# One-core attention and mixture-of-experts block: earlier value blocks, keys in three passes, and small moves between engines

## The reference, cut to what matters

```python
q = (queries @ Wq + bq); k = (keys @ Wk + bk); v = (values @ Wv + bv)   # keys = values = the context
scores = where(causal, -inf, q @ k.T);  attn = softmax(scores * scale)
x = x + (attn @ v) @ Wo + bo            # queries = layernorm(x)
# second block, on u = layernorm(x)
qkv = layernorm(u) @ qkv_weight.T;  ao = softmax(causal(q @ k.T * scale)) @ v
h1 = u + ao @ proj_weight.T
logits = layernorm(h1) @ router_weight          # top 2 of 8, capacity 1280 an expert
moe = scatter_add(prob * (gelu(token @ w1) @ w2))
out = x + (h1 + moe)
```

## Time and profile before

| | us |
|---|---|
| median of 3 runs | 1589.51 |
| lowest, highest | 1587.81, 1590.07 |
| profiled execution | 1583.6 |
| its span | 1581.8 |
| mean granted TensorE clock | 0.976 of full speed |

### The profile page before, as it was taken

The page is one execution under the profiler, slowest core; times in us unless marked ns, Lnnn a source line. Parts: engine busy times, 40 slices in busy tenths (PEclk is TensorE's granted clock), DMA queues, the critical chain, the costliest instruction groups (busy, mean ns, idle before and its releaser), DMA issues. The chain is left out here.

```text
span 1581.8 us, 31078 instructions
## 1 busy us (share of the span) xinstructions
PE 1477.9 (93%) x11056; PEld 1309.9 (83%) x11057; DVE 920.4 (58%) x1741; ACT 712.1 (45%) x1425; POOL 833.5 (53%) x951
## 2 busy tenths in 40 slices
PE   8798899999999999899859998999999899999986
PEld 6577788888888888788749988998999789899876
DVE  3767677777778767788665464433233653453361
ACT  2445545555555555565415453433233643342341
POOL 2445455556666556698725566542542855354332
PEclk9999999999999999999959999999999999999999
DMA  7212211122222111222223343432422534333222
GB/s 262 66 63 75 88 59 50 63 72 82 75 75 67 62 66 64 75 93 88 99 80 91 78 88 100 104 83 54 107 58 48 135 90 103 81 94 54 32 35 25
DMA packets 64400, 125.96 MB, mean 80 GB/s; under 512 B 13369, under 2 KB 13785, under 8 KB 63724
## 3 DMA queue, kind: packets, MB, share of 16 engines
q1 hardware_dynamic: 45932, 93.81, 18.2%
q0 software_dynamic: 17920, 29.31, 10.9%
q10 hardware_dynamic: 384, 0.61, 0.1%
HBM read 89.14 MB, written 46.27 MB: 86 GB/s over the span
## 5 line engine op out<-in xcount | busy, mean ns | idle before, releaser
L1503 PEld LDWEIGHTS hidden_ps<-gT,w 128*128 128x128 f32 x2880 | 350.3, 192 | 11.3 <-ACT hT L1408 3.9
L1503 PE MATMUL hidden_ps<-gT,w 128*128 128x256 f32 x2880 | 352.9, 284 | 7.0 <-ACT hT L1408 3.5
L1530 PE MATMUL expert_ps<-w,hT 128*128 128x512 f32 x1440 | 341.0, 396 | 8.1 <-DVE og L1458 8.1
L1530 PEld LDWEIGHTS expert_ps<-w,hT 128*128 128x128 f32 x1440 | 271.9, 191 | 65.9 <-DVE og L1458 8.9
L1283 POOL TENSOR_TENSOR w<-raw,w 128x1024 fp32r<-128x1024 f32 x62 | 152.9, 2514 | 261.5 <-ACT w L1277 261.5
L1433 DVE TENSOR_TENSOR hT<-gl,hT 128x512 fp32r<-128x512 f32 x160 | 125.9, 795 | 249.0 <-ACT hT L1408 225.3
L1406 ACT ACTIVATE gl<-hidden_ps 128x512 f32<-128x512 f32 x160 | 95.7, 598 | 326.6 <-PE hidden_ps L1503 258.6
L1387 POOL DMA_INDIRECT out_dram<-og,idx x78 | 126.0, 1616 | 72.8 <-DVE og L1458 44.0
L1458 DVE TENSOR_SCALAR og<-expert_ps,kept 128x512 f32<-128x512 f32 x80 | 59.3, 749 | 156.4 <-PE expert_ps L1530 147.4
L1416 ACT ACTIVATE gT<-yk 128x256 fp32r<-128x256 f32 x160 | 67.0, 419 | 127.7 <-DVE yk L1444 118.7
L1375 POOL DMA_INDIRECT xg<-normed_tokens,idx x78 | 86.4, 1108 | 56.2 <-POOL idx L1370 30.9
(11 more groups left out here) (184 smaller groups left out, 3079.5 us busy)
## 6 DMA issues: line engine op xcount, KB each, us to landing
raw<-L_ffn_moe_w_dram SPq DMA_DIRECT2D x64, 512.0 KB
normed_tokens<-h SPq DMA_DIRECT2D x128, 65.0 KB
xa<-x_dram SPq DMA_DIRECT2D x32, 256.0 KB, 2.7
xc<-x_dram SPq DMA_DIRECT2D x32, 256.0 KB, 3.0
attended_rows<-x SPq DMA_DIRECT2D x32, 256.0 KB, 2.1
fx<-attended_rows SPq DMA_DIRECT2D x128, 64.0 KB
out_dram<-fx SPq DMA_DIRECT2D x128, 64.0 KB
fx<-qkv_rows_dram SPq DMA_DIRECT2D x1, 1536.0 KB, 6.7
```

The lines of the kernel that those rows point to most:

```text
L1503: last = pe.matmul(pH[:, q, f * W:(f + 1) * W], w1[p][l][:, k, cols], xT[g.s % 2][r][:, k, :], start=k == 0 and n == 0, stop=k == KT - 1 a ...
L1530: last = pe.matmul(pY[:, k, :], hT[par][l][:, f, k * P:(k + 1) * P], w2[p][r][:, f, :], start=f == 0 and n == 0, stop=f == FT - 1 and n == 2)
```

## The change

Nine things are changed.

1. The keys are made in three fp32r passes. ScalarE copies the high halves of each of the four parts of cT and rk into the buffers that later hold wqkv and wpj, VectorE makes the low halves, and TensorE issues 96 matmuls. This stands ahead of the statistics and norms of the first tiles on VectorE and ScalarE.
2. A table VALUES sets where the value blocks are made: blocks 0 and 1 in step 2 (0 ahead of q, 1 ahead of "s"), block 2 in step 3, blocks 3 and 4 in step 4 (3 ahead of "xt", 4 ahead of "s"). Their banks are 4, 5, 4, 6, 5. SyncE sends them one step later, now behind xc.
3. A job that takes banks 0 or 1 from scores waits for the first half of pr alone.
4. In the odd steps 5 to 13 ScalarE copies pT ahead of xT_hi, and VectorE makes the low half of xT, in the steps before these, behind the sums of the exponentials.
5. The pieces of wpj and wqkv are prepared in the other order, wpj first.
6. In steps 15 to 38 VectorE transposes q of the second attention ahead of the softmax sum and its reciprocal.
7. In the steps after 38 v_spread is made by ScalarE (4 copies with a scale), not by GpSimd.
8. The choice of tiles 26 to 30 moves from step 50 to step 49, behind the maxima.
9. The low half of the last piece of the first expert's first weights moves from VectorE in step 50 to GpSimd in the expert phase.

```diff
-LATE_LOW = {LATE + 11: 6, LATE + 12: 7}
+LATE_LOW = {LATE + 11: 6}
 VB = -(-S * SK // P)
-CHOICES = {..., STEPS - 2: (26, 31, None)}
+VALUES = {2: ((0, 0), (1, 2)), 3: ((2, 2),), 4: ((3, -1), (4, 2))}
+VALUE_BANKS = (4, 5, 4, 6, 5)
+CHOICES = {..., STEPS - 3: (26, 31, None)}
...
+    cTh = [w[:, :, 0:S * SK] for w in wqkv]
...
         def bank_free(pe, kind, t, j=0):
             for old, t_old, j_old in ousted[kind, t, j]:
-                pe.wait_ge(*read_out[old](t_old, j_old))
+                if old == "s" and kind != "s" and place[kind, t, j] < 2:
+                    pe.wait_ge(s["shifted"], 2 * t_old + 1)
+                else:
+                    pe.wait_ge(*read_out[old](t_old, j_old))
...
# SyncE
                 if 0 < i < NT - 2:
                     load_x(i + 2)
-                b = i - 3
-                if 0 <= b < VB:
+                t = tile(i, LP)
+                if t is not None:
+                    need(sp, s["x2_done"], t - 1)
+                    sp.dma_start(xc[:, t % 2, :], x2d[row0(t):row0(t) + P, :]).then_inc(xc_in[t % 2], 16)
+                for b, _ in VALUES.get(i - 1, ()):
                     sp.wait_ge(s["val_done"], b + 1)
                     for seq, row, key, n in value_rows(b):
                         sp.dma_start(va[key:key + n, seq, :, :]..., stage[row:row + n, :]).then_inc(va_in[b], 16)
...
# GpSimd
                 f = tile(i, FF + 2)
-                if f is not None:
+                if f is not None and i <= LATE:
                     pool.wait_ge(s["v_kept"], f + 1)
...
+                if isinstance(c, int) and c == 0 and i == 5:
+                    low(pool, 0, 0, CH - 1)
...
# ScalarE
+            for k in range(KT):
+                act.wait_ge(keys_in[k], 32)
+                act.activation(cTh[0][:, k, :], cT[:, k, :], ACT.Copy)
+                act.activation(wpj[0][:, k, :], rk[:, k, :], ACT.Copy).then_inc(s["key_hi"], 1)
             for t in range(2):
                 norm_x(t)
...
+                turned_first = i % 2 == 1 and LP <= i <= FF
+                if not turned_first:
+                    normed_high(i)
...                                        # here the copies of pT
+                if turned_first:
+                    normed_high(i)
...
+                f = tile(i, FF + 2)
+                if f is not None and i > LATE:
+                    act.wait_ge(s["v_kept"], f + 1)
+                    act.wait_ge(s["v_spread"], f)
+                    need(act, s["o2_mm"], f)
+                    for b in range(4):
+                        last = act.activation(vbd[:, :, b, :], vn[:, f % 2, :]..., ACT.Copy, scale=blocks[:, b:b + 1])
+                    last.then_inc(s["v_spread"], 1)
...
# VectorE
-            for t in range(2):
-                stats_x(t)
+            for k in range(KT):
+                dve.wait_ge(s["key_hi"], k + 1)
+                dve.tensor_tensor(cTh[1][:, k, :], cT[:, k, :], cTh[0][:, k, :].bitcast(F32), ALU.subtract)
+                dve.tensor_tensor(wpj[1][:, k, :], rk[:, k, :], wpj[0][:, k, :].bitcast(F32), ALU.subtract)\
+                   .then_inc(s["key_lo"], 1)
+                if k % 2 == 1:
+                    stats_x(k // 2)
...
-                b = i - 2
-                if 0 <= b < VB:
+                for b, _ in VALUES.get(i, ()):
                     dve.wait_ge(s["val_mm"], b + 1)
                     dve.wait_ge(bias_in, 32)
                     if b > 0:
...
                     dve.transpose(hq, parts(bank("qkv", f, 0))).then_inc(s["q_turned"], 1)
+                f = tile(i, FF + 2)
+                if f is not None and i <= LATE:
+                    dve.wait_ge(s["exp2"], f + 1)
+                    need(dve, s["shared2"], f - 1)
+                    chained(dve.tensor_reduce(den2[:, :], p2, X, ALU.add))
+                    dve.reciprocal(rec2[:, f % 2, :], den2[:, :]).then_inc(s["rec2_done"], 1)
...
# TensorE
+            def values(i, stage):
+                for b, at in VALUES.get(i, ()):
+                    if at == stage:
+                        pe.wait_ge(wv_in, 16)
+                        bank_free(pe, "val", b)
...
             for k in range(KT):
-                pe.wait_ge(keys_in[k], 32)
-                for n in range(8):
...
+                pe.wait_ge(s["key_hi"], k + 1)
+                for n_pass, (w, c) in enumerate(PASSES):
+                    if n_pass == 1:
+                        pe.wait_ge(s["key_lo"], k + 1)
+                    for n in range(8):
...
```

More of the change, by code:

```diff
@@ L182, in psum_jobs, with values @@
     fz, fq, fs, fo, ft, fr = (tile(i, FF + n) for n in range(6))
-    jobs = [("xt", tx, 0, 1)] + [("pt", tp, j, 0) for j in range(4)] + [("p2t", fo, 0, 0)]
+    def values(stage):
+        return [("val", b, 0, 1) for b, at in VALUES.get(i, ()) if at == stage]
+    jobs = values(-1) + [("xt", tx, 0, 1)] + [("pt", tp, j, 0) for j in range(4)] + [("p2t", fo, 0, 0)]
+    jobs += values(0)
     if i % 2 == 0:
@@ L201, in own_bank @@
         return 2
-    if kind in ("pt", "val"):
+    if kind == "val":
+        return VALUE_BANKS[t]
+    if kind == "pt":
         return 4 + j % 2
@@ L1027, in _ @@
                         dve.reciprocal(rec[:, t % 2, heads], den[:, heads]).then_inc(s["rec_done"], 1)
+                if i % 2 == 0 and LP <= i + 1 <= FF:
+                    later(i + 1)
                 if i > FF:
@@ L1045, in turn_z @@
                 transposes("zt", f, z).then_inc(s["zt_mm"], 1)
+            def values(i, stage):
[3 more added lines that the diff above has]
+                        bank_free(pe, "val", b)
+                        n = min(P, S * SK - P * b)
+                        for k in range(KT):
+                            last = pe.matmul(bank("val", b)[0:n, :], cT[:, k, P * b:P * b + n], rv[:, k, :],
+                                             start=k == 0, stop=k == KT - 1)
+                        last.then_inc(s["val_mm"], 1)
             def count_places(a, b, batches):
@@ L1063, in _ @@
             for k in range(KT):
-                pe.wait_ge(keys_in[k], 32)
-                for n in range(8):
-                    m, h = divmod(n, 2)
-                    last = pe.matmul(bank("key", n)[:, 0:HC], rk[:, k, m * P:(m + 1) * P], cT[:, k, h * HC:(h + 1) * HC],
-                                     start=k == 0, stop=k == KT - 1)
-                    if k == KT - 1:
-                        last.then_inc(s["key_mm"], 1)
+                pe.wait_ge(s["key_hi"], k + 1)
[3 more added lines that the diff above has]
+                    for n in range(8):
+                        m, h = divmod(n, 2)
+                        final = k == KT - 1 and n_pass == 2
+                        last = pe.matmul(bank("key", n)[:, 0:HC], wpj[w][:, k, m * P:(m + 1) * P],
+                                         cTh[c][:, k, h * HC:(h + 1) * HC], start=k == 0 and n_pass == 0, stop=final)
+                        if final:
+                            last.then_inc(s["key_mm"], 1)
             pe.wait_ge(small_in, 16)
@@ L1129, in _ @@
                     count_places(*COUNTS[i])
-                b = i - 2
-                if 0 <= b < VB:
-                    pe.wait_ge(wv_in, 16)
-                    bank_free(pe, "val", b)
-                    n = min(P, S * SK - P * b)
-                    for k in range(KT):
-                        last = pe.matmul(bank("val", b)[0:n, :], cT[:, k, P * b:P * b + n], rv[:, k, :],
-                                         start=k == 0, stop=k == KT - 1)
-                    last.then_inc(s["val_mm"], 1)
+                values(i, 2)
                 if tq is not None:
```

45 lines of the change are left out of this document (25 added, 20 removed).

## The result

| | kernel before | changed kernel |
|---|---|---|
| median of 8 runs | 1588.11 us | 1593.71 us |
| lowest, highest | 1585.10, 1590.35 | 1590.84, 1594.78 |
| profiled execution, span | 1583.6, 1581.8 | 1593.6, 1591.8 |

The changed kernel is slower: ratio 1.0032, interval 1.0022 to 1.0042, some 5.1 us. The forecast was 3.4 us faster, and the time lies just outside its range. The two spans differ by 10.0 us, twice what the medians do, since the profiled execution of the kernel before is a short one, 4.5 us under its median. A comparison of the two traces has to be brought down by some 4.5 us, and the traces do not say where.

The account below looks back on a forecast made before the run. TensorE, busy 93%, bounds the kernel, so only its stops pay. Early +9.4, steady −8.6, late −1.6, end −2.6 make −3.4 on 1583.6 us; with 5.9 us to the median carried over, 1586.1 us, range 1580 to 1593.

Parts of the forecast that it names:

- The new wait, twice: Steps 2 and 4: VectorE's second value addition waits for the first block's DMAs; stalls of 6.3 and 8.2 us.
- rivals A and B: A: values' DMAs don't hold VectorE, sum −19.4, 1570 us, chance 0.08. B: transfers land sooner, −5.7, 1583.8, chance 0.17.
- The start: From the keys to s of the first value step: keys done 2.1 us sooner, but s 4.2 us later.
- rival C: TensorE falls to the lower clock behind each new stop: +7.7, sum +4.3, 1593.8 us, chance 0.17.
- The half shift: Early steps: q's first half waits for half of pr only, which gives 0.79 us each time.
- the early part: All up to the second attention's begin: start, two stalls and what comes back, +9.4 us in sum.
- The steady steps: Second attention: q's transposition moved ahead of reduction and reciprocal lets all 15 pv waits go, −8.6 us.
- rival D: The reorder gives half, as z_lo or an xT_lo takes the transposition's place: +4.3, sum +0.9, 1590.4, chance 0.18.
- The late steps: v_spread on ScalarE shortens h1's norm from 1.27 to some 0.55 us; with two pj waits gone, −1.6 us.
- The end: Between last logits and last maxima, a low half (1.25 us) and ten choice operations (2.2 us) go elsewhere: −2.6 us.
- The low half goes to GpSimd's idle time: The end: GpSimd, busy 53%, takes the low half of weights; without that idle time at least 1.25 us come back.

Follow-up runs that it names:

- the first experiment: Changed kernel with two buffers for the value blocks in turn, so no addition waits for the DMAs of the block just before; 1571.57 us, ratio 0.9905.

## Why the prediction was wrong

**The new wait, twice: right.** It named the buffer, the two additions, the DMAs and TensorE's stops, and even "released by a DMA of va". From the end of s to the mask it took 6.9 us in step 2 (44.48 to 51.35), forecast 6.3, and 7.6 in step 4 (76.20 to 83.76), forecast 8.2. The two landings took 5.7 us (from the transposition's end, 45.07, to the addition) and 5.3 (from the load at 77.83), forecast 5.1 and 5.9, so rivals A and B are out. Two buffers give 20 us and one block a step 18; the forecast had 16 us for the two stalls with their clock.

**The start: the first failed term.** I had the first value block start at 27.0 and take 3.60 us, and q take 5.8, as if TensorE kept its clock across a stop of 3.9 us. The stop was 3.60 us. The mask came at 51.35, not at 47.5. Of these some 3.9 us, 0.9 is the block's later start (27.91), 2.2 the block itself (5.8 us to the start of q at 33.72), 0.3 q (6.1 us) and 0.6 the landing. The later start comes from the keys: I had 14 us for the 96 matmuls, they took 16.2 (7.03 to 23.27), and were done 0.6 us sooner than before, not 2.1.
The lower clock behind the stops is rival C, which I gave 0.17: the window rows show it behind all three, under 0.8 over 21.6 us of the first 100, its own sign. C's prices were too high, 7.7 us. The chain lost 2.2 and 0.3 us behind the first stop, 1.1 behind the second (14.4 us from the mask to q of step 4 against 13.3, inside the +1.5 that I allowed) and 0.9 behind the third (14.2 us to q of step 6 against 13.3), 4.5 in all. So it is luck that C's 1593.8 us is the measured time: the other part of that time lies in the expert phase, of which C says nothing.
At q of step 6 the changed kernel is 18.5 us late (97.95 against 79.48), forecast 14.8. The half shift, the blocks gone from steps 5 and 6 and the waits of q (4.9 to 0.5 us) came as worked out: from there to q of step 10 the lateness falls by 4.9 us, forecast 5.1. So the early part is +13.6 instead of +9.4.

**The steady steps: right.** −9.4 by the traces and −9.2 by its own run, forecast −8.6; z_lo's 0.8 us of slack held, and no wait of pv or qkv on another line came in between 270 and 580 us: rival D is out.

**The late steps: right in sign.** By the traces they gave 0.8 us of the 1.6 forecast; the undoing of v_spread on ScalarE says about 3 (unclear by the intervals). The 1.27 us of h1's norm that I read was one of the long ones: in the steps from 700 us on the nine take 0.70 us on average before and 0.54 in the changed kernel.

**The end: right, and more than all of it paid back.** The chain starts sooner as forecast, by 3.3 us in the traces (forecast 2.6), and by about 2 us with the low half alone moved, where TensorE's waits on the last choices fall from 3.1 and 0.5 to 1.1 us. "The low half goes to GpSimd's idle time" was the second failed term: I looked at GpSimd's idle time and not at what VectorE does in it. VectorE's two low halves took 3.41 us instead of 1.00, and TensorE stood 2.6 us; with the same low half on VectorE the stop is gone. The page of the Trainium skill that I had quoted in the late steps, "SBUF — State Buffer" (Who interferes with whom), says that VectorE and GpSimd share a pair of ports under an exclusive lock. The trace agrees: 3.41 us. I applied it to the operation taken off GpSimd and not to the one put on it.

**Not foreseen: the expert phase.** The stretch of the second matmuls is 5.2 us longer by trace (715.7 to 720.9). My sum had nothing for it. With the keys alone undone it is 716.5 us, 4.4 less, but the medians differ by about 1.5 only. Why three-pass keys lengthen it stays open.

Together, by the lateness of the same matmuls in the two traces:

| part | forecast | traces |
|---|---|---|
| early, to 264 us | +9.4 | +13.3 |
| steady steps, to 593 us | −8.6 | −9.4 |
| late steps, to 790 us | −1.6 | −0.8 |
| the end, to 824 us | −2.6 | −3.3 |
| first group of the experts, to 856 us | 0 | +5.0 |
| the rest | 0 | +5.2 |
| sum | −3.4 | +10.0 |

The medians differ by 5.1, not 10.0; some 4.5 of it are the short profiled execution of the kernel before, and the table does not say in which row. By the medians, moving the low half costs 1 to 2 us as a whole (the kernel before with it alone, the changed kernel without it); it gains about 2.2 at the end, so it costs some 3 to 4 in the first group of the experts. The wrong sign comes from the first row and from the two rows that I had at nothing. Items 3, 4, 5 and 8 of the change were not run alone.

## What to carry to other kernels

A table that puts two producers of one buffer into one step needs a second buffer, or a step between them: count, for each buffer, the time from the last write to the landing of what empties it, and what is queued ahead of those DMAs. Price what follows a stop of some microseconds once at either clock, if the trace has one such stretch, as this one had, and carry the difference as a range. When work goes to an idle engine, look at what its neighbour does in that interval, not at its own idleness.

## What the runs showed of the hardware

TensorE's granted clock was 0.57, 0.67 and 0.56 in the 6 to 8 us behind stops of 3.60, 7.66 and 5.75 us, and 1.00 again in 97.95 to 104.00. The length of the stop does not decide it alone: behind a stop of 3.59 us the same block of 8 matmuls took 5.37 us in the first experiment, behind 2.91 us it took 3.67, and behind the same stop of 1.62 us in the late steps the clock was 0.78 in one kernel and 1.00 in another.

A low half of 128x256 on VectorE takes 0.42 us; two beside a 128x1024 one on GpSimd took 3.41 us. GpSimd's took 2.35 us, no more than its average of 2.50 over 63 of them, so here it was VectorE that waited.

The same expert code took 715.7 to 727.0 us in the profiled executions of seventeen kernels, by what stood ahead of it or by the execution. Shown by medians is one step of it: 5.6 us, 0.35%, between three-pass and full keys, with the start equal within 0.2 us by trace. Where stops by issue come and go, as here, a difference of 0.3% between two programs can lie in code that was not touched.
